# Two slots instead of four in the closing sum over the expert outputs

## The reference

```python
mod = (silu(c) @ wmod).reshape(16, 6, 1, -1)
sa, ca, ga, sb, cb, gb = (mod[:, k] for k in range(6))
ga, gb = (clip_away_from_zero(g, 0.25) for g in (ga, gb))
h = layernorm(x) * (1 + ca) + sa
x = x + ga * gather_conv(h)                    # 32 taps per token and head, weights looked up in 64 bins
h = layernorm(x) * (1 + cb) + sb
scores = h @ gate_w.T                          # 8 experts
topk_scores, topk_idx = top_k(scores, 2)
p = softmax(topk_scores)
y = sum(p[k] * (silu(h1) * h2) @ w3[topk_idx[k]].T for k in range(2))   # h1, h2 = halves of h @ w12[expert].T
x = x + gb * y
```

## Time and profile before

| | |
|---|---|
| median of 3 runs | 1384.0 us (1383.26 to 1384.48) |
| time of the profiled execution | 1384.0 us |
| its span | 1382.2 us |
| busy over the span: TensorE | 1147.0 us, 83% |
| VectorE | 1035.7 us, 75% |
| ScalarE | 929.3 us, 67% |
| GpSimd | 709.7 us, 51% |
| last scatter instruction of the second stage starts | 1342.39 us |
| first fetch issued | 1344.76 us |
| VectorE's first and last instruction of the closing sum start | 1349.74 and 1377.84 us |

### The profile page before, as it was taken

How to read it: one execution, slowest core, us unless ns; L and a number is a source line. 1 busy time by engine, 2 the same in 40 slices (tenths; PEclk the granted TensorE clock), 3 DMA queues, 4 the chain that set the end, 5 groups by cost and what they waited for, 6 DMA issues and landing times.

```text
span 1382.2 us, 34969 instructions
## 1 busy us (share of the span) xinstructions
PE 1147.0 (83%) x11339; PEld 780.6 (56%) x11339; DVE 1035.7 (75%) x2314; ACT 929.3 (67%) x1905; POOL 709.7 (51%) x906
## 2 busy tenths in 40 slices
PE   0569998999999899999989989999951699999970
PEld 0346666665666666666666656666641365556540
DVE  1279899989999998998999899889945233333338
ACT  0268888888878877887887887878730255555540
POOL 4335227456745745774584477446344544545440
PEclk9989999999999999999999999999985799999995
DMA  5345535545544554554455446444440262222228
GB/s 161 107 137 149 145 102 150 154 133 145 144 147 123 156 160 124 142 160 137 118 166 149 128 132 162 121 125 137 126 144 23 79 189 76 70 71 72 69 64 347
DMA packets 213344, 181.27 MB, mean 131 GB/s; under 512 B 147632, under 2 KB 183344, under 8 KB 212272
## 3 DMA queue, kind: packets, MB, share of 16 engines
q1 hardware_dynamic: 204496, 161.12, 41.1%
q0 software_dynamic: 8672, 17.92, 3.8%
HBM read 96.86 MB, written 82.12 MB: 129 GB/s over the span
## 4 chain that ended last, share of the span: by engine, by line
PE 50%; DVE 10%; issue 9%; POOL 7%; ACT 4%; DMA 1%; another core or an unknown queue 1%; DVEq 0%; SPq 0%; POOLq 0%; ACTq 0%
PE ps L989 10%; PE ps L1131 8%; PE ps L1009 6%; PE ps L976 5%; DVE aw L1294 4%; PE ps L981 4%; PE ps L1146 4%; PE ps L1031 2%; PE ps L996 2%; PE ps L1138 2%; PE ps L943 2%; PE ps L1019 2%; ACT att L785 1%; PE ps L1125 1%; POOL y_scratch L707 1%
## 5 line engine op out<-in xcount | busy, mean ns | idle before, releaser
L777 ACT ACTIVATE ee<-ps,f 128x512 f32<-128x512 f32 x512 | 354.5, 693 | 121.1 <-PE ps L976 117.1
L1294 DVE TENSOR_TENSOR aw<-dq,ks 128x520 f32<-128x520 int32 x512 | 417.3, 815 | 2.7 <-DMA ks<-k_scratch 2.7
L1284 DVE SCALAR_TENSOR_TENSOR dq<-ps,ee 128x512 int32<-128x512 f32 x512 | 350.1, 684 | 44.5 <-PE ps L981 38.4
L989 PE MATMUL ps<-ident,aw 128*128 128x128 f32 x2048 | 314.5, 276 | 39.0 <-ACT att L785 22.6
L989 PEld LDWEIGHTS ps<-ident,aw 128*128 128x128 f32 x2048 | 239.1, 141 | 183.3 <-issue 65.7
L785 ACT ACTIVATE att<-ps 128x512 f32<-128x512 f32 x512 | 310.3, 606 | 20.4 <-PE ps L989 18.4
L617 POOL COPY kn<-kn 128x256 f32<-128x256 f32 x64 | 25.4, 396 | 353.5 <-DVE kn L1274 348.5
L981 PE MATMUL ps<-cn,ptt 128*128 128x512 bf16 x512 | 195.2, 382 | 9.8 <-DVE dq L1284 9.5
L976 PE MATMUL ps<-cp,ptt 128*128 128x512 bf16 x512 | 197.2, 386 | 0.0
L707 POOL DMA_INDIRECT y_scratch<-aw,idu x135 | 129.1, 956 | 129.5 <-ACT aw L868 121.0
L586 POOL DMA_INDIRECT slot_scratch<-hrow,spotu x128 | 139.7, 1092 | 46.7 <-issue 33.4
(11 more groups left out here) (178 smaller groups left out, 1676.9 us busy)
## 6 DMA issues: line engine op xcount, KB each, us to landing
k_scratch<-kn SPq DMA_DIRECT2D x64, 512.0 KB, 3.1
ka<-e_scratch SPq DMA_DIRECT2D x64, 512.0 KB
ks<-k_scratch SPq DMA_DIRECT2D x128, 130.0 KB
e_scratch<-kr SPq DMA_DIRECT2D x128, 126.0 KB, 3.4
dl<-slot_scratch SPq DMA_DIRECT2D x135, 65.0 KB
xc<-in_x SPq DMA_DIRECT2D x8, 512.0 KB, 5.9
h_scratch<-hx SPq DMA_DIRECT2D x16, 256.0 KB, 3.9
hgr<-h_scratch SPq DMA_DIRECT2D x8, 512.0 KB, 5.1
```

The lines of the kernel that those rows point to most:

```text
L777: act.activation(ee[:, T % ERING, :], ps_p[T % 2][:, :], ACT.Relu, scale=f27[:, i % 2, r, h:h + 1]).then_inc(s_e, 1)
L989: last = nc.tensor.transpose(bank[:, j * P:j * P + P], aw[:, T % RING, o:o + P], ident[:, :])
L1284: nc.vector.scalar_tensor_tensor(dq[:, T % DRING, o:o + 512], ps_n[T % 2][:, :], SCALE, ee[:, T % ERING, :], ALU.mult, ALU.add).then_inc(s ...
L1294: nc.vector.tensor_tensor(aw[:, T % RING, :].rearrange("p (g k) -> p g k", k=8), dq[:, T % DRING, :].rearrange("p (g k) -> p g k", k=8), r ...
```

## The change

The ring of the closing sum gets two slots instead of four. `FRING` goes. The inputs of the two slots stay where slots 0 and 1 were (in `att`), the outputs in the two halves of `ka`; `kn` and `ee` are no longer used here. SyncE fetches pairs 0 and 1 at first, and after `store(f)` it issues `fetch(f + 2)` instead of `fetch(f + 4)`. The semaphores `s_xf` and `s_out` go from four to two each. VectorE's three instructions for a pair are the same in form and size; its wait for the slot's earlier store now comes from f = 2 on instead of f = 4.

```diff
-FRING = 4
...
-        y12 = [att[:, 0:8, :].rearrange("p a n -> p (a n)").rearrange("p (k s n) -> p k s n", k=2, s=2),
-               flat.rearrange("p (k s n) -> p k s n", k=2, s=2)]
+        y1 = att[:, 0:4, :].rearrange("p a n -> p (a n)").rearrange("p (s n) -> p s n", s=2)
+        y2 = att[:, 4:8, :].rearrange("p a n -> p (a n)").rearrange("p (s n) -> p s n", s=2)
...
-        xf = [ka[:, n, :, :].rearrange("p h k -> p (h k)") for n in range(2)]
-        xf += [ee[:, 2 * n:2 * n + 2, :].rearrange("p a n -> p (a n)") for n in range(2)]
+        xf = ka[:, :, :, :].rearrange("p s h k -> p s (h k)")
...
-            def fetch(f):
-                s = f % FRING
-                for k in range(TOP):
+            def fetch(f, s):
+                for k, dst in enumerate((y1, y2)):
                     o = (k * PAIRS + f) * RES * P
-                    sp.dma_start(y12[s // 2][:, k, s % 2, :], yscr[o:o + RES * P, :].rearrange("(p r) c -> p (r c)", r=RES)).then_inc(s_xf[s], 16)
+                    sp.dma_start(dst[:, s, :], yscr[o:o + RES * P, :].rearrange("(p r) c -> p (r c)", r=RES)).then_inc(s_xf[s], 16)
...
-            for f in range(FRING):
-                fetch(f)
+            fetch(0, 0)
+            fetch(1, 1)
             for f in range(PAIRS):
                 store(f)
-                if f + FRING < PAIRS:
-                    fetch(f + FRING)
-            for n in range(FRING):
-                sp.wait_ge(s_out[n], 16 * len(range(n, PAIRS, FRING)))
+                if f + 2 < PAIRS:
+                    fetch(f + 2, f % 2)
+            for n in range(2):
+                sp.wait_ge(s_out[n], 16 * PAIRS // 2)
...
-                s = f % FRING
...
-                dve.wait_ge(s_xf[s], 32 * (f // FRING + 1))
-                if f >= FRING:
-                    dve.wait_ge(s_out[s], 16 * (f // FRING))
...
+                s = f % 2
+                dve.wait_ge(s_xf[s], 32 * (f // 2 + 1))
+                if f >= 2:
+                    dve.wait_ge(s_out[s], 16 * (f // 2))
```

More of the change, by code:

```diff
@@ L280, in build @@
         s_ys = [sem(f"expert_scattered{n}") for n in range(YRING)]
-        s_xf = [sem(f"pair_fetched{n}") for n in range(FRING)]
+        s_xf = [sem(f"pair_fetched{n}") for n in range(2)]
         s_xm = sem("kept_rows_loaded")
         s_sum, s_o = sem("sums_ready"), sem("out_ready")
-        s_out = [sem(f"out_stored{n}") for n in range(FRING)]
+        s_out = [sem(f"out_stored{n}") for n in range(2)]
         consts = [(tokpos[:], c_tok), (ident[:], c_ident), (iota[:], c_iota), (trif[:], c_tri.rearrange("k p m -> p k m")),
@@ L460, in kept_in @@
                     sp.dma_start(xm[f], xscr[f, :, :]).then_inc(s_xm, 16)
-            def fetch(f):
-                s = f % FRING
-                for k in range(TOP):
+            def fetch(f, s):
+                for k, dst in enumerate((y1, y2)):
                     o = (k * PAIRS + f) * RES * P
-                    sp.dma_start(y12[s // 2][:, k, s % 2, :], yscr[o:o + RES * P, :].rearrange("(p r) c -> p (r c)", r=RES)).then_inc(s_xf[s], 16)
+                    sp.dma_start(dst[:, s, :], yscr[o:o + RES * P, :].rearrange("(p r) c -> p (r c)", r=RES)).then_inc(s_xf[s], 16)
             def store(f):
                 sp.wait_ge(s_o, f + 1)
-                sp.dma_start(oflat[f, :, :], xf[f % FRING]).then_inc(s_out[f % FRING], 16)
+                sp.dma_start(oflat[f, :, :], xf[:, f % 2, :]).then_inc(s_out[f % 2], 16)
             sp.wait_ge(s_tab, 1)
@@ L1463, in _ @@
             for f in range(PAIRS):
-                s = f % FRING
-                both12, o = y12[s // 2][:, :, s % 2, :], xf[s]
-                by_token = o.rearrange("p (r c) -> p r c", c=C)
-                dve.wait_ge(s_xf[s], 32 * (f // FRING + 1))
-                if f >= FRING:
-                    dve.wait_ge(s_out[s], 16 * (f // FRING))
-                link(nc.vector.tensor_tensor(o, both12[:, 0, :], both12[:, 1, :], ALU.add))
-                link(nc.vector.tensor_tensor(by_token, by_token, rows(gbm[:, f, :], [[0, RES], [1, C]]), ALU.mult))
-                nc.vector.tensor_tensor(o, o, xm[f], ALU.add).then_inc(s_o, 1)
+                s = f % 2
+                dve.wait_ge(s_xf[s], 32 * (f // 2 + 1))
+                if f >= 2:
+                    dve.wait_ge(s_out[s], 16 * (f // 2))
+                link(nc.vector.tensor_tensor(xf[:, s, :], y1[:, s, :], y2[:, s, :], ALU.add))
+                link(nc.vector.tensor_tensor(xf[:, s, :].rearrange("p (r c) -> p r c", c=C), xf[:, s, :].rearrange("p (r c) -> p r c", c=C),
+                                             rows(gbm[:, f, :], [[0, RES], [1, C]]), ALU.mult))
+                nc.vector.tensor_tensor(xf[:, s, :], xf[:, s, :], xm[f], ALU.add).then_inc(s_o, 1)
 def kernel(**inputs):
```

## The result

| | before | changed |
|---|---|---|
| median of 9 runs | 1384.5 us (1383.2 to 1391.9) | 1398.3 us (1393.1 to 1401.4) |
| ratio | | 1.0083, interval 1.0060 to 1.0106 |
| profiled execution, its span | 1384.0, 1382.2 us | 1404.7, 1402.9 us |
| closing sum, first add's start to last add's end | 29.32 us | 40.08 us |
| of it, VectorE idle | 0 | 10.1 us |

The forecast was 1389.4 us, 5.4 us more, with a range to 1392.5. The direction was right, the size was not. By the ratio the change costs 8 to 15 us; the closing sum of the profiled execution is 10.8 us longer.

A forecast was written before the change was run, and what follows sets the result against it. VectorE, busy without a gap in the closing sum, was taken as the bound. Three stalls of 1.77 us (5.31) plus about 0.1 for pair 7 gave 1384.0 + 5.4 = 1389.4 us, range 1387.1 to 1392.5.

The forecast's parts named there:

- What bounds the stage: Closing sum: wholly on the critical path, VectorE busy without a gap at 3.66 us a pair, DMA engines near second.
- The round trip, steps 1 to 4: Closing sum: store issue, store landing, first and second fetch transfer; fetch lands 5.25 us after the pair's end.
- step 3: First fetch transfer lands 4.0 us after the pair's end at the earliest; the store ahead would give 3.9.
- E: End of a pair's last add on VectorE, from which the prediction counts issues and landings.
- step 4: Second fetch transfer lands 1.25 us behind the first, at E + 5.25, set by the engines, not its issue.
- The three of a pair take 3.75 us: DMA engines in the closing sum: a store and two fetch transfers per pair, 1.25 us each at 420 GB/s.
- Bounds: Fetch landing in the closing sum: E + 4.87 (1388.2 us), by issue alone E + 4.5 (1387.1), at most E + 6.16 (1392.2).
- The edits at nothing: Output-slot wait, fewer semaphores and end waits, moved buffers, load on the DMA engines: costed at nothing; nothing moves ahead.
- the hidden fetch: Rival: the fetch flies while the other pair is worked on, so no stall in the closing sum; 1384.0 us, chance 0.07.
- the crowded opening: Rival: four opening transfers instead of eight, so VectorE starts the closing sum 0.9 us sooner; 1383.1 us, chance 0.02.
- The dearer round trip: Rival: the fetch's read starts only once the store is through; landing E + 6.16, 1392.2 us, chance 0.14.
- The change does bind: Answers the rival that it does not: SyncE issuing the fetch before the store would start it 0.4 us earlier; no chance given.

The follow-up runs named there:

- e7: Changed kernel with four output slots instead of two; closing sum 40.2 us, ratio to the kernel before 1.0075.
- e9: Changed kernel run again without an edit; closing sum 39.4 us, ratio to the kernel before 1.0064.
- e13: Like e5, but 128 of each pair's 1024 columns (64 KB) stored ahead of the fetch; closing sum 36.5 us, ratio to the kernel before 1.0070.
- e1: Kernel before with one slot instead of four; closing sum 71.5 us, ratio to the kernel before 1.0308.
- e5: Changed kernel with results written over the residual and all stores issued behind the last fetch; closing sum 35.0 us, ratio to the kernel before 1.0056.
- e14: Like e5, but an unused 512 KB load from HBM ahead of each fetch; closing sum 42.3 us, ratio to the kernel before 1.0114.
- e6: Changed kernel with each fetch issued ahead of the store and four output slots; closing sum 36.6 us, ratio to the kernel before 1.0055.
- e3: Changed kernel with each fetch issued ahead of the store, two output slots; closing sum 43.6 us, ratio to the kernel before 1.0094.
- e8: Changed kernel with the fetch issued after the pair's first add, ahead of its store, and four output slots; closing sum 32.0 us, ratio to the kernel before 1.0018.
- e2: Kernel before with three slots instead of four; closing sum 31.0 us, ratio to the kernel before 1.0017.
- e4: Changed kernel with the fetch issued after the pair's first add, ahead of its store; closing sum 36.7 us, ratio to the kernel before 1.0052.
- e11: Changed kernel with stores issued by ScalarE on its own queue; closing sum 38.6 us, ratio to the kernel before 1.0050.

## Why the prediction was wrong, point by point

- **What bounds the stage**: right. The closing sum is on the path with every us; all of the loss is VectorE idle in it (10.1 of 10.8 us; the rest is the overlap of two adds lost at each stall).
- **The round trip, steps 1 to 4**: this term failed. I had 5.25 us; measured are 5.9 with one slot, and with two, over three profiles (changed, e7, e9), 6.1 to 6.8 for the even pairs and 6.1 to 8.0 for the odd ones. The step that failed is step 3, the first transfer of the fetch: E + 4.0 there, E + 5.1 in the changed kernel; the 1.25 of step 4 held (1.2). Step 3 took the later of two landings, the lone fetch's and the one behind the store, where a good part of them adds: I let the store's transfer vanish in the latency of the fetch. With only 64 KB ahead and the issue as in the changed kernel, the fetch lands at 5.5 (e13), 0.3 above my figure, and the rest of the store's bytes adds 0.4 (e1) to 0.8 (pair 2 of the changed kernel). My upper bound of 6.16, which added the whole 1.25 of the store, was nearly right for the even pairs.
- **"The three of a pair take 3.75 us"**: this is what put the odd pairs wrong. I let fetch 3 queue behind fetch 2 at 420 GB/s and found it ready in time, no stall beyond 0.1. That rate is one of a queue that never empties. With two pairs' transfers under way and holes between them, the landing for pair 3 came 4.5 us after that for pair 2, that for pair 5 6.3 after that for pair 4. The odd pairs are the path. From the end of pair 1, 3 or 5 to the first add of the pair after next it took 7.20, 8.05 and 6.19 us, where I had 5.44, 5.35 and 5.35: 1.8, 2.7 and 0.8 more, together the 5.3 us by which the profile's sum passed mine (10.8 less 5.4). Had all three been as short as the last, 2.4 us of the 5.3 would stand; this much is the round trip's, and the other 2.9 are what pairs 3 and 5 lost beyond it. That the bytes under way are behind it is shown by e5 and e13 (4.9 and 5.8 for pair 3) against e14 (7.7). That they are not all of it is shown by e6, where the same bytes in another order kept the 3.75, and by the nearly idle engines before the two landings. How the neighbour's transfers do it stays open.
- **Bounds**: both were built for a pair whose neighbour does not disturb it. A bound on one round trip is no bound on a chain of them; the upper end had no term for what neighbouring slots cost each other, and the range ended at 1392.5.
- **The edits at nothing**: right. Stores landed ahead of the fetches (e7), adds took 1.22 to 1.23 us, nothing ahead of the stage moved (e9).
- **Rivals**: the hidden fetch and the crowded opening fell as argued; the opening fetch took 4.8 us with two transfers behind it (4.9 in e7 and e9), where it had taken 4.9 with six. The dearer round trip, given 0.14, was the nearest in its number; its mechanism, a read that starts only once the store is through, does not fit e6, where the fetch is nearly as late with the store behind it. The change does bind: with the fetch ahead of its store (e3, e6) the kernel is slower than the kernel before as well.
- **The formula of the Trainium skill** ("DMA: Bandwidth & Descriptors", Anatomy of one DMA), which the page fits for the path of GpSimd, had given an estimate of 5.6 us for three transfers, nearer to the 5.9 of e1 than my 5.25. I set it aside as its fixed part did not fit a single store. For the fetch alone it gives an estimate of 2.0 + 2.4 = 4.4 us, where e5 shows 5.1 for pair 2 and 4.8 to 4.9 for pairs 3 to 5. So the traces lie above it for two and three transfers, and below it for a single store (2.6 us, not 3.2).

## What to carry to other kernels

A rate read where the queue is full must not be used where the change empties it: with a short queue, each batch pays its start, its holes and its tail (4.8 us for three transfers in e1, not 3.75), and the batches of neighbouring slots can delay each other (up to 8.0 us for a round trip of 6.2). The depth of a ring is judged by the whole round trip, from the release of the buffer to the landing, against the work on the other slots (here 6 to 8 us against 3.7); releasing the input as soon as it is read (e8, 32.0 us) buys nearly as much as a third slot (e2, 31.0). When the order of transfers in a queue is changed, every wait on what now stands behind must be looked at again (e3, e4).

## What I had not expected of the hardware

- Order in the queue hardly protects the fetch for pair 2, which meets idle engines: a store of 512 KB behind the fetch cost it 0.8 us (e6 against e5), one ahead of it 0.4 to 0.8 beyond its issue, and one issued at the same moment from another engine's queue 1.2 us (e11). For the odd pairs it did make a difference (e6 against e7), and I have no reason for it.
- The fetch for pair 5 took 6.9 to 7.1 us from the issue of its second transfer in three profiles of this order (changed, e7, e9), against 5.2 to 5.9 for the even pairs. Longer sharing with fetch 4 fits, since store 3 is issued 1.5 to 1.7 us before fetch 4 lands, but the overlap for pair 3 is longer (2.4 to 2.6 us) and costs less. What stands behind differs too: store 4 and the next fetch are issued while fetch 5 is still under way, by 2.3 to 2.6 us, against 0.6 to 1.2 for what stands behind fetch 3, but that is in part a result of its lateness. And the engines as a whole moved only 49 GB/s in the half microsecond from 1383.5, 2 us before it landed (41 at the same place in e7, 148 in e9). Why just here is open; it was not tried.
- The start of the closing sum moved by up to 10 us between executions that have the same instructions ahead of it (first fetch at 1344.4 to 1354.8 us in all groups but that of e1 to e4, 1328.4 to 1329.2 there). What causes it is open, too.
